# Causal attention with ALiBi: scores, mask add and exp of the diagonal key tiles limited to the query columns that the later product reads

## What is computed

```python
# x: [B, 4096, 1024], 16 query heads, 4 key/value heads, head size 64
q = (x @ Wq.T).reshape(B, L, N_KV, Q_PER_KV, HEAD_DIM)
kv = (x @ Wkv.T).reshape(B, L, N_KV, 2, HEAD_DIM)
qk = SCALE * einsum('blgpd,bmgd->bgplm', q, k)
qk = qk + slopes[:, None, None] * tril(pos[None, :] - pos[:, None])[None]
qk = where(pos[None, :] <= pos[:, None], qk, -inf)
out = softmax(qk) @ v          # per head
return out @ Wo.T
```

## Time and profile before

| | us |
|---|---|
| timed runs | 8411.3 and 8693.34, median 8552.32 |
| profiled execution | 8425.03 |
| its span, slowest core (core 7) | 8423.5 |
| spans of the 8 cores | 8352.2 to 8423.5 |
| TensorE busy in the span | 6481.8 (77%) |
| VectorE busy | 2409.4 (29%) |
| ScalarE busy | 1849.1 (22%) |
| mean granted TensorE clock | 0.796 |

### The profile page before, as it was taken

One profiled execution on the slowest core, in us unless ns is written; L12 is line 12 of the kernel. 1 busy time (PEld: TensorE's weight loads), 2 busy tenths in 40 slices (PEclk: granted clock), 3 DMA queues, 4 the chain that ended last, 5 costly groups with the idle time before them and its releaser, 6 DMA issues.

```text
span 8423.5 us, 94217 instructions; the slowest of 8 cores (8352.2 to 8423.5 us)
## 1 busy us (share of the span) xinstructions
PE 6481.8 (77%) x32824; PEld 3046.6 (36%) x32824; DVE 2409.4 (29%) x5754; ACT 1849.1 (22%) x2914; POOL 380.2 (5%) x702
## 2 busy tenths in 40 slices
PE   0188898968898888984677777778768887888788
PEld 0034444423343333432333333434433333333333
DVE  0133333232223222222543332131223322233222
ACT  0011111210011000110245544646541100111010
POOL 1000000000000000000000000000000000000000
PEclk9976687679999999996655555555559999999899
DMA  9700010033433434333000000000012333433333
GB/s 117 95 21 21 21 41 21 11 111 130 150 116 140 145 130 150 115 138 93 21 21 21 1 21 21 1 21 8 4 51 109 147 136 129 144 124 148 125 133 128
DMA packets 167315, 689.34 MB, mean 82 GB/s; under 512 B 14512, under 2 KB 45360, under 8 KB 125904
## 3 DMA queue, kind: packets, MB, share of 16 engines
q0 software_dynamic: 132880, 548.84, 21.1%
q1 hardware_dynamic: 33984, 134.48, 4.5%
HBM read 661.59 MB, written 98.60 MB: 90 GB/s over the span
## 4 chain that ended last, share of the span: by engine, by line
PE 70%; DMA 8%; DVE 8%; issue 6%; another core or an unknown queue 4%; ACT 3%; DVEq 1%; ACTq 0%; POOLq 0%; SPq 0%
PE pf L1021 13%; PE pf L1030 13%; PE pf L1306 10%; PE pf L1093 9%; DMA f_w2s<-ffw 6%; PE pf L412 4%; PE pf L1343 4%; PE pf L432 3%; ACT b_PT L1327 2%; PE pb L389 1%; PE pf L611 1%; PE pf L740 1%; DVE pf L1316 1%; DVE xn L381 1%
## 5 line engine op out<-in xcount | busy, mean ns | idle before, releaser
L1093 PE MATMUL pf<-f_w2s,f_H1G 128*128 128x512 bf16 x5120 | 1168.6, 385 | 243.5 <-DMA f_w2s<-ffw 180.7
L1327 ACT ACTIVATE b_PT<-pf,alibi_sb 128x512 bf16<-128x512 f32 (+2 forms) x1657 | 1089.6, 661 | 748.6 <-PE pf L1306 601.6
L1021 PE MATMUL pf<-xnT,f_w1s 128*128 128x512 bf16 x5120 | 1224.7, 382 | 0.0
L1030 PE MATMUL pf<-xnT,f_w3s 128*128 128x512 bf16 x5120 | 1210.6, 379 | 0.3
L1306 PE MATMUL pf<-b_QT,b_Kz 128*128 128x512 bf16 (+2 forms) x1657 | 924.6, 558 | 248.0 <-DVE b_Vaug L1236 0.7
L1093 PEld LDWEIGHTS pf<-f_w2s,f_H1G 128*128 128x128 bf16 x5120 | 490.7, 99 | 921.4 <-issue 392.1
L1343 PE MATMUL pf<-b_Vaug,b_PT 128*128 128x65 bf16 x5565 | 619.7, 245 | 221.9 <-ACT b_PT L1327 221.7
L1040 ACT ACTIVATE f_sA<-pf 128x512 bf16<-128x512 f32 x640 | 382.1, 597 | 1754.8 <-PE pf L1021 1754.4
L1030 PEld LDWEIGHTS pf<-xnT,f_w3s 128*128 128x128 bf16 x5120 | 500.8, 98 | 607.1 <-issue 21.9
L1021 PEld LDWEIGHTS pf<-xnT,f_w1s 128*128 128x128 bf16 x5120 | 493.6, 99 | 609.3 <-issue 46.2
L1343 PEld LDWEIGHTS pf<-b_Vaug,b_PT 128*128 128x128 bf16 x5565 | 485.0, 126 | 560.1 <-issue 521.6
(11 more groups left out here) (186 smaller groups left out, 4551.2 us busy)
## 6 DMA issues: line engine op xcount, KB each, us to landing
f_w1s<-ffw POOLq DMA_DIRECT2D x160, 1024.0 KB, 5.2
f_w3s<-ffw POOLq DMA_DIRECT2D x160, 1024.0 KB, 7.4
f_w2s<-ffw POOLq DMA_DIRECT2D x320, 512.0 KB, 3.7
Xa<-xout SPq DMA_DIRECT2D x16, 2048.0 KB
xf<-Xa SPq DMA_DIRECT2D x16, 2048.0 KB
xf<-x SPq DMA_DIRECT2D x8, 2048.0 KB
ffw<-f_w POOLq DMA_DIRECT2D x16, 1024.0 KB, 47.4
Xb<-xout SPq DMA_DIRECT2D x8, 2048.0 KB
```

Of the source, the lines that this page charges most:

```text
L1021: slot=slot: t.matmul(pA_["t"][:, 0:CH], w1s[:, sl, ic, 128 * hc:128 * hc + 128], xnT[slot][:, ic, :], start=(ic == 0), stop=(ic == 7)),
L1030: slot=slot: t.matmul(pB_["t"][:, 0:CH], w3s[:, sl, ic, 128 * hc:128 * hc + 128], xnT[slot][:, ic, :], start=(ic == 0), stop=(ic == 7)),
L1093: pos=pos, a_=accs[j]: t.matmul(a_["t"][:, 0:512], H1G[:, e, hc, 128 * j:128 * j + 128], w2s[:, sl, hc, :], start=(pos == 0 and hc == 0), ...
L1327: s.activation(PTs[ki % 4][:, 0:qc], pS["t"][:, 0:qc], AF.Exp, bias=alibi_sb[:, col:col + 1]),
```

## The change

For a key tile on the diagonal the first query columns are wholly masked, and `b_pv` never reads their exp. The change computes `j0`, the first column that `b_pv` reads, and starts the score matmul, the mask add and the exp there instead of at column 0:

```diff
+                                j0 = 128 * max(0, (128 * kt - q0 - qw + 128) // 128)
                                 mS = k.op("t", lambda t, ...: t.matmul(
-                                              pS["t"][:, 0:qc],
+                                              pS["t"][:, j0:qc],
                                               Kz[:, g, 128 * kt:128 * kt + 128],
-                                              QTb[:, s_, qci * qc:qci * qc + qc],
+                                              QTb[:, s_,
+                                                  qci * qc + j0:qci * qc + qc],
                                               start=True, stop=True,
                                               skip_group_check=True), inc=True)
-                                if 128 * kt + 127 >= q0:
+                                if 128 * kt + 127 >= q0 + j0:
                                     k.wait("v", "t", mS)
-                                                    pS["t"][:, 0:qc], pS["t"][:, 0:qc],
-                                                    tri_bf[:, 512 + q0 - 128 * kt:
+                                                    pS["t"][:, j0:qc],
+                                                    pS["t"][:, j0:qc],
+                                                    tri_bf[:, 512 + q0 - 128 * kt + j0:
                                                            512 + q0 - 128 * kt + qc],
-                                               PTs[ki % 4][:, 0:qc], pS["t"][:, 0:qc],
+                                               PTs[ki % 4][:, j0:qc],
+                                               pS["t"][:, j0:qc],
                                                AF.Exp, bias=alibi_sb[:, col:col + 1]),
```

More of the change, by code:

```diff
@@ L1300, in b_scores @@
                             def b_scores(ki, kt, q0=q0, qci=qci, qc=qc, g=g, s_=s_,
-                                         base=base, h=h):
+                                         base=base, h=h, qw=qw):
+                                j0 = 128 * max(0, (128 * kt - q0 - qw + 128) // 128)
                                 pS = pool.acquire()
@@ L1304, in b_scores @@
                                 k.wait("t", "s", m_q)
-                                mS = k.op("t", lambda t, g=g, s_=s_, kt=kt,
+                                mS = k.op("t", lambda t, g=g, s_=s_, kt=kt, j0=j0,
                                           q0=q0, qci=qci, qc=qc, pS=pS: t.matmul(
-                                              pS["t"][:, 0:qc],
+                                              pS["t"][:, j0:qc],
                                               Kz[:, g, 128 * kt:128 * kt + 128],
-                                              QTb[:, s_, qci * qc:qci * qc + qc],
+                                              QTb[:, s_,
+                                                  qci * qc + j0:qci * qc + qc],
                                               start=True, stop=True,
@@ L1312, in b_scores @@
                                 pS["wmark"] = mS
-                                if 128 * kt + 127 >= q0:
+                                if 128 * kt + 127 >= q0 + j0:
                                     k.wait("v", "t", mS)
-                                    mtri = k.op("v", lambda v, kt=kt, q0=q0, qc=qc, pS=pS:
-                                                v.tensor_tensor(
-                                                    pS["t"][:, 0:qc], pS["t"][:, 0:qc],
-                                                    tri_bf[:, 512 + q0 - 128 * kt:
+                                    mtri = k.op("v", lambda v, kt=kt, q0=q0, qc=qc,
+                                                j0=j0, pS=pS: v.tensor_tensor(
+                                                    pS["t"][:, j0:qc],
+                                                    pS["t"][:, j0:qc],
+                                                    tri_bf[:, 512 + q0 - 128 * kt + j0:
                                                            512 + q0 - 128 * kt + qc],
@@ L1325, in b_scores @@
                                 col = al_cols[(h, 128 * kt - q0 - qc // 2)]
-                                msx = k.op("s", lambda s, qc=qc, col=col, ki=ki, pS=pS:
-                                           s.activation(
-                                               PTs[ki % 4][:, 0:qc], pS["t"][:, 0:qc],
+                                msx = k.op("s", lambda s, qc=qc, col=col, ki=ki,
+                                           j0=j0, pS=pS: s.activation(
+                                               PTs[ki % 4][:, j0:qc],
+                                               pS["t"][:, j0:qc],
                                                AF.Exp, bias=alibi_sb[:, col:col + 1]),
```

## The result

The changed kernel takes 0.9894 of the time of before, 95% interval 0.9874 to 0.9913: 1.1% faster, which at a resolution of 2% is no change. Its profiled execution took 8317.5 us against 8425.0. The median of its 11 timed runs is 8579.5 us (8320.0 to 8832.5), that of the 10 runs of before 8638.0; both medians lie well above the lowest runs because in many executions of either kernel some cores were granted a lower clock, and the ratio leaves those out.

A forecast was written before the change was run, and what follows sets the result against it. It took the order of small dependent steps through TensorE, VectorE and ScalarE, not a full engine, to bound the attention. 74.9 + 5.7 = 80.6 us off the profiled 8425.0 gave 8344 us, range 8300 to 8480.

The forecast's parts named there:

- the two chains: From score 3 to the next block: through VectorE's mask add and queued scalings, or through ScalarE's exp 3 and PV 3.
- Tiles 0 to 2: First three diagonal tiles of a 512-query block: shorter scores gain nothing, PV 0 waits for exp 0; 0.32 us without that.
- Tile 3: Last diagonal tile: score 0.32 and mask add 0.40 us shorter, exp adds nothing; 0.72 us a block, 74.9 us over 104.
- The 256 heads: 32 blocks of 256 queries, last tile cut to 128 columns: 3.5 to 7.8 us, middle 5.7 taken.
- The lower bound of the sum: All blocks set by exp alone: 0.32 us each over 104 blocks plus 3.5, 37 us.
- held elsewhere: Rival: next block's start does not move with the shorter mask add on VectorE's queue; only 37 us, 8388; chance 0.09.
- The sum: Whole attention stage: 74.9 us from tile 3 plus 5.7 from the 256 heads, 80.6 us saved.
- The rule on the columns: Skill's pricing of TensorE matmuls: columns over 1.2 GHz, 0.64 us a 512 block, 70 us in all.
- a median placed as that of before is: Upper end of the range: median 127 us over the profiled execution, 8344 + 127 = 8471, so it ends at 8480.
- Columns only: Rival: stage gains as if TensorE streamed without stop, 0.64 us a 512 block, 70 us, 8355; chance 0.07.
- both rivals on the clock: Projections lose the fast clock (8608, slower), or the clock rises inside the attention (near 7950); chance 0.02 each.
- Both add up: Rival: score 3 moves forward too, so scores 1 and 2 also pay; 116 us, 8309; chance 0.08.

The follow-up runs named there:

- parts by single operation: Changed kernel with only the score, only the mask add or only the exp narrowed: 2160.5, 2156.0 and 2191.0 us first to last score, 2199.6 before.
- xblock3: Changed kernel with scores and PV in one queue across block ends, PV three tiles behind: 7835.7 us at the lowest, ratio 0.932 to the kernel before.
- xblock3_full: Schedule of xblock3 with full width on every diagonal tile, the change undone: 7930.4 us at the lowest, ratio 0.9418 to the kernel before.
- tail_early_after: Changed kernel with the previous block's closing issued behind the third key tile: 2054.6 us first to last score, 2110.5 for the changed kernel.
- xblock: Changed kernel with the two-tile distance between scores and PV kept across block ends: 1819 us first to last score, 8034 us in all.
- depth3_after: Changed kernel with PV three tiles behind the scores instead of two: 2036.4 us first to last score, 2110.5 for the changed kernel.

## Why the prediction was right, and where it was wrong

**What bounds the stage, and the two chains.** Right. The intervals forecast for a block were 2.90 and 2.59; the trace has 2.90 and 2.58 for the block that was read. (Over the stage 3.31 and 3.44 us are both common before, and 2.59 and 2.72 after; the difference is 0.72 in either case.) The parts by single operation (39, 44 and 9 us) show each term of the 0.72 us and the zero for the exp.

**Tiles 0 to 2 are worth nothing, exp 0 is the cover.** Right: 0 in the ordinary blocks when changed alone, 0.32 us when the cover is gone.

**Tile 3, 0.72 us a block.** Right for 96 of 104 blocks. Wrong for head 3: its predecessor is a block with 256 queries and has two scalings to do, not four, 0.48 us instead of 0.86. There PV 3 is last, and the three savings add to 1.04. The next lines are the end of such a block (chunk 5, head 3) in the changed kernel:

```profile
5188.91 0.26 PE L1307 MATMUL pf<-b_QT,b_Kz 128*128 128x128 bf16 x1
...
5189.72 0.48 DVE L1255 TENSOR_SCALAR b_tok<-pf,b_rec 128x64 bf16<-128x64 f32 x2
...
5190.24 0.22 PE L1347 MATMUL pf<-b_Vaug,b_PT 128*128 128x65 bf16 x1 [0.48 <-ACT b_PT L1330]
5190.38 0.42 PE L1265 MATMUL pb<-idn_bf,b_tok 128*64 128x128 bf16 x2
```

The transposes follow PV 3 at once, 0.18 us after the scalings ended at 5190.20. I read one block of a large chunk and one of chunk 0, both behind a block of their own kind; that missed 2.4 us.

**The 256 heads.** The bounds 0.11 to 0.24 us were too low: most of these blocks gave 0.26 to 0.29 (8.2 us together instead of 5.7). The lower bound counted the exp alone, but the chain through exp also holds the score and the mask add ahead of it, so it shortens by all three, 0.11 + 0.13 + 0.11 = 0.35. The measured value lies between the two chains.

**The lower bound of the sum.** It had the same slip: "a block in which exp alone sets the next start gains 0.32 us". Exp 3 waits for mask add 3, and that for score 3, so such a block gains 1.04, as head 3 shows. The 37 us of the rival "held elsewhere" cannot be had from that mechanism.

**The sum.** 80.6 us forecast, 89.1 measured: 2.4 more from head 3, 2.5 more from the small blocks, 0.7 less since the last block ends behind the last score, and 4.3 from blocks with a table load and from scatter between the chunks, which I did not count.

**The rule on the columns.** The Trainium skill (TensorE: Matmul & The Clock Gate, "Back-to-back issue gap") would have had 70 us for the changed kernel. The trace does not agree: the stage's gain is a latency through two engines. Where no block's end is left (xblock3 against xblock3_full), chunks 0 and 3 differ by 7.6 us each, and that pricing gives 8.7: there it comes near.

**The predicted time and range.** This is the step that failed: "a median placed as that of before is, 127 us over its profiled execution". I took that distance from a median of two runs, and it was itself a half-way value between a low and a high one. Ten runs put the median of before at 8638.0, 213 us over its profiled execution, and the changed kernel's median at 262 over its own (8579.5 - 8317.5). The term that was mis-sized is that distance, 127 for 262; with it the working gives 8344 + 262 = 8606. The forecast time itself, 8344, had this distance at nothing. The difference between the kernels, which is what the profile can tell, was 1.0% forecast and 1.1% measured.

**The rivals.** Columns only (70 us), held elsewhere (37) and both rivals on the clock did not come about. The clock did rise in the attention of xblock3, where the waits were taken away, but not by the narrower tiles. Both add up (116) is what the change is worth once PV 0 no longer waits (116.3 measured), not as the kernel stood.

## What to carry to other kernels

Cutting work off the instructions of a dependent chain pays at the places where the chain is late, and there it pays the full latency of every engine on the chain, not the busy time of the busiest one: of 0.64 us of columns saved per block 0.32 was worth something, and 0.40 came from an engine that is busy a sixth of the time in the last chunks. List the chains that meet at the wait, with their slack, for each kind of block, since the one that comes second takes over as soon as the first is shortened. And look at the end of a software-pipelined block before narrowing anything inside: here keeping the pipeline running across blocks, with PV three tiles behind, was worth 5.8% by itself (xblock3_full, a good part of it by the clock), the narrower tiles 1.1%, and both together 7%.

## What the runs showed of the hardware that I had not expected

The granted clock of TensorE in this stage cannot be told from the busy share that a profile shows. In chunk 6 the changed kernel has TensorE busy 230 of 295 us, 78%, at 0.50, the 1.2 GHz level; xblock3 has it busy 147 of 194 us, 76%, at 0.92. The runs in between take the waits away by parts. The same chunk, first with the previous block closed earlier (tail_early_after), then without ends of blocks but PV two tiles behind (xblock, core 4):

```profile
5441.00:5729.00 288.00, 226.07 (x1373) 124.78 (x1372) 53.51 (x165) 187.04 (x294) 0.00 (x0) 0.50 0.00 1
```
```profile
5329.00:5568.00 239.00, 188.10 (x1374) 111.50 (x1373) 53.04 (x164) 182.10 (x294) 0.00 (x0) 0.66 0.00 1
```

With only the wait for exp 0 gone (depth3_after) the chunk is at 0.50 too, busy 228 of 286 us, and so are the other seven, to 0.01. With only the ends of the blocks gone (xblock) it has 0.66, and with both gone (xblock3) 0.92. So the wait for exp 0 alone does not hold the clock down, the ends of blocks matter more, and the two together most. What decides inside the stage stays open, since the order of the work alone does not settle it either: xblock3 has the same order in chunks 3 and 4, granted 0.56 and 0.53. Its 0.92 is a mean of the two levels: in chunk 6 the first 32 us, the short blocks of the first heads, are at 0.50 (5204 to 5236 us, TensorE busy 24.1 of 32), the 161 us behind them at 1.00 (busy 121.9).

The Trainium skill (TensorE: Matmul & The Clock Gate, "A second HAM failure mode: psum-queue depth-cycling") describes a kernel in which short idle times between groups of matmuls make the clock swing between its two levels. The trace agrees in part: xblock swings between them in chunk 6 (0.66: at 0.50 from 5446 to 5483 us, at 1.00 from 5484 to 5497), but the changed kernel, with more idle time, stays at the lower level throughout.
